# Setup of an attention block reordered: first batch normalised ahead of the second's statistics, later second queries, 40 banks of row maxima for 44

## The reference

```python
x = x + tanh(g_xattn) * xattn(layernorm(x), ctx, ctx, Wq, Wk, Wv, Wo)   # 16 heads of 8, 154 keys
x = x + tanh(g_ffn) * moe(layernorm(x), Wr, W1, b1, W2, b2)             # 8 experts, top 2, capacity 160
# xattn: softmax(where(tril, q k^T / sqrt(8), -inf)) v, then Wo
```

## Time and profile before

| | us |
|---|---|
| three timed runs | 143.20, 143.31, 143.89 |
| span of the profiled execution | 141.4 |
| PE busy / DVE busy / POOL busy / ACT busy | 125.7 / 104.8 / 85.0 / 72.9 |

### The profile page before, as it was taken

How to read it: one execution, slowest core, us unless ns; L and a number is a source line. 1 busy time by engine, 2 the same in 40 slices (tenths; PEclk the granted TensorE clock), 3 DMA queues, 4 the chain that set the end, 5 groups by cost and what they waited for, 6 DMA issues and landing times.

```text
span 141.4 us, 2256 instructions
## 1 busy us (share of the span) xinstructions
PE 125.7 (89%) x723; PEld 86.9 (61%) x723; DVE 104.8 (74%) x261; ACT 72.9 (52%) x129; POOL 85.0 (60%) x126
## 2 busy tenths in 40 slices
PE   5998988999899999999999669989979999989940
PEld 2443844456455646665258556979769999977620
...
DMA packets 19018, 12.22 MB, mean 86 GB/s; under 512 B 3381, under 2 KB 16999, under 8 KB 19008
## 3 DMA queue, kind: packets, MB, share of 16 engines
q1 hardware_dynamic: 17344, 9.59, 26.5%
...
q10 hardware_dynamic: 576, 0.66, 1.3%
...
...
## 4 chain that ended last, share of the span: by engine, by line
PE 34%; POOL 21%; issue 15%; DMA 11%; DVE 11%; ACT 2%; POOLq 2%; SPq 2%; DVEq 0%
POOL slots L536 8%; PE turn L833 6%; PE av L889 4%; DVE top L1242 4%; POOL results L568 4%; PE turn L846 3%; DMA xn_all<-results 3%; PE av L897 3%; PE sc L1120 3%; DMA X<-x 2%; PE sc L865 2%; PE turn L852 2%; DMA parts_all<-slots 2%; POOL shared L457 2%; DMA slots<-rows,slot_of 2%
## 5 line engine op out<-in xcount | busy, mean ns | idle before, releaser
L1242 DVE TENSOR_REDUCE top<-turn 128x3 fp32r<-128x462 f32 (+2 forms) x44 | 26.2, 606 | 14.1 <-PE turn L833 7.2
L568 POOL DMA_INDIRECT results<-p,result_of x18 | 19.8, 1101 | 12.9 <-DVE p L1526 8.0
L659 ACT ACTIVATE p_all<-sc 128x1024 f32<-128x1024 f32 x16 | 15.5, 1022 | 16.2 <-PE sc L865 16.1
L536 POOL DMA_INDIRECT slots<-rows,slot_of x16 | 19.4, 1211 | 6.0 <-issue 5.0
L833 PE MATMUL turn<-shared,q_all 128*128 128x462 f32 (+2 forms) x44 | 20.4, 469 | 2.3 <-DVE top L1242 0.8
L1120 PE MATMUL sc<-q_all,w_all 128*128 128x320 f32 x96 | 17.4, 320 | 1.3 <-issue 1.3
L716 ACT ACTIVATE late<-sc,B 128x320 f32<-128x320 f32 x32 | 14.9, 521 | 4.2 <-PE sc L1120 4.2
L1120 PEld LDWEIGHTS sc<-q_all,w_all 128*128 128x128 f32 x96 | 14.2, 188 | 2.3 <-issue 2.1
L833 PEld LDWEIGHTS turn<-shared,q_all 128*128 128x128 f32 x44 | 8.3, 189 | 11.3 <-ACT q_pack_all L625 4.7
L527 POOL TENSOR_SCALAR_AFFINE_SELECT p_all<-p_all 128x512 f32<-128x512 f32 x8 | 5.2, 645 | 16.8 <-ACT p_all L659 16.8
L1543 DVE TENSOR_TENSOR shared<-late,shared 128x640 fp32r<-128x640 f32 x16 | 13.1, 821 | 0.3
...
## 6 DMA issues: line engine op xcount, KB each, us to landing
...
```

The source lines that it names most:

```text
L536: nc.gpsimd.indirect_dma_start(out=slots, out_offset=bass.IndirectOffsetOnAxis(ap=slot_of[:, c:c + 1], axis=0), in_=rows[:, t, :], in_offs ...
L568: nc.gpsimd.indirect_dma_start(out=results, out_offset=bass.IndirectOffsetOnAxis(ap=result_of[0:m, e, n:n + 1], axis=0), in_=y[0:m, e % 2, ...
L659: act.activation(p0[:, t, heads, :], sc[:, heads, :], ACT.Exp, scale=SCALE).then_inc(sc_free, 1)
L1242: dve.tensor_reduce(top[:, qt, h0:h0 + nh, 3 * HD], ps[:, 0:nh * keys].rearrange("p (h k) -> p h k", h=nh), AX.X, ALU.max).then_inc(turn_f ...
```

## The change

1. VectorE normalises the first batch before it takes the second's statistics, each tile with its own signal, and TensorE transposes tile by tile. The first batch's input comes in two halves, on two queues.
2. The second batch's rows are normalised by GpSimd (4 instructions), between two pieces of masked keys. Their transposes move behind the first packing, the projection behind turn 0's last score product, and its high and low parts into turn 0.
3. The high keys are written straight from PSUM by ScalarE, with no copy in between. VectorE masks four heads' keys instead of six; GpSimd makes heads 4 to 9, then 10 to 15.
4. `slot0` and the ones beside the values are written by VectorE instead of GpSimd. The mask of the last keys is 32 x 32 and is spread by a repeated identity.
5. Units: three heads wherever possible, and head 3 of query tiles 1 to 3 in one joined bank. That is 20 banks per batch for 22; setup does 5 units instead of 7. The three units that start at head 7 stand behind turn 0's packing.
6. Fills of TensorE ahead of the first queries: 3 and 3 instead of 12 and 4.

Core of the diff:

```diff
+def units_of_maxima(b, i):
+
+    first = [(b, (0,), 4 * i, 4, P)]
+    if i == 0:
+        return first + [(b, (qt,), 0, 3, C) for qt in range(1, QT)] + [(b, tuple(range(1, QT)), 3, 1, C)]
+    starts = ((), (4, 7), (10,), (13,))[i]
+    return first + [(b, (qt,), h0, 3, C) for h0 in starts for qt in range(1, QT)]
...
-        shares = (7, 8, 6, 6, 6, 5, 5, 1)
+        maxima_todo = [u for b in range(B) for i in range(4) for u in units_of_maxima(b, i)]
+
+        shares = (5, 7, 6, 6, 6, 5, 4, 1)
         maxima_first = maxima_todo[:shares[0]]
-        FIRST_HEADS = 6
+        FIRST_HEADS = 4
+        NEXT_HEADS = 10
...
@@ -403,10 +406,8 @@
                 ins.then_inc(pool_step, 1)
                 pool.wait_ge(pool_step, steps[0])
...
+            pool.wait_ge(cleared, 1)
+            packing(pack_k, [kp for kp, qp in PRODUCTS]).then_inc(pack_ready, 1)
+            pool.tensor_copy(identb[:, :], identf[:, :]).then_inc(consts2, 1)
+            root((0, QT), 1)
             step(pool.memset(mask_q[:, :, :], 0.0))
             pool.affine_select(out=mask_q[:, :, :], in_=mask_q[:, :, :], compare_op=ALU.is_ge, fill=NEG,
-                               base=0, pattern=[[0, 4], [-1, P]], channel_multiplier=1)
+                               base=0, pattern=[[0, 4], [-1, P]], channel_multiplier=1).then_inc(consts2, 1)
             pool.tensor_copy(identr[:, :], identf[:, :])
-            pool.tensor_copy(identb[:, :], identf[:, :]).then_inc(consts2, 1)
-            root((0, QT), 1)
-            root((QT, NT), 2)
-
-            pool.wait_ge(cleared, 1)
-            packing(pack_k, [kp for kp, qp in PRODUCTS]).then_inc(pack_ready, 1)
+            pool.wait_ge(cleared, 2)
             packing(pack_q, [qp for kp, qp in PRODUCTS]).then_inc(pack_ready, 1)
...
+            pool.wait_ge(kT_ready, 1)
+            keys_for_max(0, FIRST_HEADS, NEXT_HEADS)
+
+            root((QT, NT), 2)
+            pool.wait_ge(rstd_ready, 2)
+            for t in range(QT, NT):
+                pool.tensor_scalar(xn[:, t, :], X[:, t, :], mean_var[:, t, 0:1], rstd[:, t:t + 1],
+                                   ALU.subtract, ALU.mult).then_inc(xn_ready, 1)
+            keys_for_max(0, NEXT_HEADS, H)
...
+            pool.memset(ident4[:, :, :], 0.0)
             step(pool.memset(mask_k1[:, :], 0.0))
-            for j in range(4):
-                m = mask_k1[32 * j:32 * j + 32, :]
-                step(pool.affine_select(out=m, in_=m, compare_op=ALU.is_ge, fill=NEG, base=0,
-                                        pattern=[[1, 32]], channel_multiplier=-1))
+            pool.affine_select(out=ident4[:, :, :], in_=ident4[:, :, :], compare_op=ALU.not_equal, fill=1.0, base=0,
+                               pattern=[[0, 4], [-1, 32]], channel_multiplier=1)
+            pool.affine_select(out=mask_k1[:, :], in_=mask_k1[:, :], compare_op=ALU.is_ge, fill=NEG, base=0,
+                               pattern=[[1, 32]], channel_multiplier=-1)
             pool.memset(ones[:, :], 1.0).then_inc(consts3, 1)
             pool.wait_ge(k_packed, 4)
...
+            act.dma_start(X[:, 2:QT, :], x_d[:, 2:QT, :]).then_inc(x_in[1], 16)
...
+            act.activation(kT_part[:, 0], sc1[:, 0:B * CP].rearrange("p (b k) -> p b k", b=B),
+                           ACT.Copy).then_inc(kT_ready, 1)
...
@@ -627,8 +627,7 @@
 
             act.wait_ge(k_packed, 4)
             pack(0)
-            act.wait_ge(small_in, 64)
-            act.activation(gate[:, :], G[:, :], ACT.Tanh).then_inc(gate_ready, 1)
+            turned_rows(1)
...
+                if g == 0:
+                    high_queries(1)
                 act.wait_ge(sc_full, 3 * g + 3)
                 act.activation(p1[:, t, :], sc1[:, 0:Q1], ACT.Exp, scale=SCALE).then_inc(sc_free, 1)
+                if g == 0:
+                    act.wait_ge(small_in, 64)
+                    act.activation(gate[:, :], G[:, :], ACT.Tanh).then_inc(gate_ready, 1)
...
-            fill(sc[:, 3, :], 12)
+            fill(sc[:, 3, :], 3)
             turn_rows(0)
-            fill(sc[:, 3, :], 4)
+            fill(sc[:, 3, :], 3)
+            pe.wait_ge(wq_in, 16)
             queries(0)
...
-            pe.wait_ge(consts2, 1)
+            pack_keys(1)
+            pe.wait_ge(consts2, 2)
             pe.wait_ge(kTr_first, 1)
             pe.wait_ge(q_high, 1)
-            maxima(maxima_first[0:2])
-            pack_keys(1)
+            maxima(maxima_first[0:1])
+            pack_keys(2)
+            maxima(maxima_first[1:2])
+            pack_keys(3)
             maxima(maxima_first[2:3])
-            pack_keys(2)
-            maxima(maxima_first[3:4])
-            pack_keys(3)
-            maxima(maxima_first[4:5])
-            turn_rows(1)
-            maxima(maxima_first[5:6])
             project_values()
-            maxima(maxima_first[6:])
-            queries(1)
+            maxima(maxima_first[3:])
             pe.wait_ge(pack_ready, 2)
             pe.wait_ge(q_ready, 1)
             pack(0)
-            pe.wait_ge(consts3, 1)
+            pe.wait_ge(v_ready, 5)
+            turn_rows(1)
             for g in range(NG + 2):
-                if g == 0:
-                    pe.wait_ge(kTr_ready, 1)
-                if g == 2:
-                    pe.wait_ge(kTr_ready, 2)
+                if g < 3:
+                    pe.wait_ge(kTr_ready, g + 1)
                 maxima(maxima_beside(g, 0))
                 if g < NG:
                     scores(g)
                 maxima(maxima_beside(g, 1))
                 if g == 0:
                     pe.wait_ge(k_ready, 1)
-                    pe.wait_ge(q_ready, 2)
+                    pe.wait_ge(consts3, 1)
                 if g < NG:
                     last_scores(g)
+                if g == 0:
+                    queries(1)
                 if g == NG + 1:
                     pe.wait_ge(sc_free, 3 * NG)
                     fill(sc[:, 0, :], 4)
@@ -1047,7 +1049,8 @@
                     pack(g + 1)
                 maxima(maxima_beside(g, 3))
                 if g == 1:
-                    pe.wait_ge(v_ready, 5)
+                    pe.wait_ge(ones_placed, 1)
+                    pe.wait_ge(q_ready, 2)
                 if 1 <= g <= NG:
                     values(g - 1)
                 maxima(maxima_beside(g, 4))
@@ -1197,7 +1200,7 @@
 
         @block.vector
         def _(dve):
...
-            dve.memset(pack_k_raw, 0.0)
+            dve.memset(pack_k_raw, 0.0).then_inc(cleared, 1)
             dve.memset(pack_q_raw, 0.0).then_inc(cleared, 1)
-            dve.wait_ge(x_in[0], 16)
-            statistics((0, QT), X)
-            dve.wait_ge(x_in[1], 16)
-            statistics((QT, NT), X)
-            layernorm((0, QT), X, xn, xn_ready)
-            dve.wait_ge(consts2, 1)
-            dve.tensor_reduce(minus_one[:, :], minus_raw[:, :, :], AX.XY, ALU.add).then_inc(minus_ready, 1)
+            step(dve.memset(slot0[:, :], 0.0))
+            dve.memset(slot0[:, D:D + 1], FAR).then_inc(slot_zeros, 1)
+            statistics((0, QT), X, True)
+
...
+            ones_beside_values()
+            dve.wait_ge(rstd_ready, 1)
+            for t in range(QT):
+                layernorm(t, X, xn).then_inc(xn_ready, 1)
...
-            dve.tensor_tensor(kT_part[:, 1], kT[:, :, :], kT_part[:, 0], ALU.subtract).then_inc(kT_split, 1)
+            dve.tensor_tensor(kT_part[:, 1], sc1[:, 0:B * CP].rearrange("p (b k) -> p b k", b=B), kT_part[:, 0],
+                              ALU.subtract).then_inc(kT_split, 1)
+            dve.wait_ge(consts1, 1)
             dve.tensor_tensor(kTr[:, 0, 0:FIRST_HEADS],
                               kT_part[:, 0, 0, 0:C].unsqueeze(1).to_broadcast([P, FIRST_HEADS, C]),
                               head_mask[:, :, :].rearrange("p i j -> p (i j)")[:, 0:FIRST_HEADS].unsqueeze(2)
                               .to_broadcast([P, FIRST_HEADS, C]), ALU.mult).then_inc(kTr_first, 1)
-            layernorm((QT, NT), X, xn, xn_ready)
+            dve.tensor_reduce(minus_one[:, :], minus_raw[:, :, :], AX.XY, ALU.add).then_inc(minus_ready, 1)
+            statistics((QT, NT), X, True)
...
             low_queries(0)
             dve.wait_ge(zeroed, 2)
             maxima(maxima_first)
             pass_bank()
-            low_queries(1)
 
             def after(k, n):
 
@@ -1463,11 +1478,16 @@
                     pass_bank()
                 for n in (3, 4, 5):
                     maxima(maxima_beside(g, n))
+                if g == 0:
+                    low_queries(1)
```

141 lines of the change are left out of this document (66 added, 75 removed).

## The result

| | before | after |
|---|---|---|
| four timed runs each on one chip, median (all), us | 143.60 (143.20, 143.31, 143.89, 144.82) | 148.38 (146.61, 147.87, 148.89, 150.73) |
| ratio after / before, 95% interval | | 1.0278 [1.0212, 1.0344] |
| span of the profiled execution, us | 141.4 | 148.5 |
| mean granted TensorE clock of the runs | 0.992 in the profiled one | 0.931, 0.945, 0.963, 0.967 |

The kernel became slower. The forecast was 142.4 (140.7 to 143.9); 148.38 lies outside its range, and "slower" had 0.13.

What follows compares the result with a forecast made beforehand. The prediction took TensorE, busy nearly throughout the head loop, as the bound, with two setup paths ahead of it. A, B, C and D: -3.1 + 0.6 + 0.85 + 0.8 = -0.85 from 143.31 gave 142.4 us (140.7 to 143.9).

Steps and rivals of the forecast that it cites:

- A: Setup path to the first scores, reordered and with fewer reductions: they start at 17.4 us against 20.48, -3.1 us.
- signs of "wrong": Third score product after 19.8 us, first reduction after 12.5, lower clock between 7 and 19, or gain staying near 3.
- B: TensorE's wait in turn 0 for GpSimd's block keys, before the third score product; +0.6 us.
- c: Price of each of GpSimd's four normalisations in setup; taken as 0.40 us, with 0.29 and 1.20 also considered.
- break-even, c = 0.61: Price of a GpSimd normalisation from which rival (3) decides, at a wait of 1.45 us.
- upper bound of c, 1.20 us: Highest price for a GpSimd normalisation, from a select beside VectorE's normalisation; TensorE would wait 3.8 us.
- C: Second batch's projection moved into the loop, behind turn 0's third score product; +0.85 us, ends 0.1 and 1.1.
- D: 924 columns of maxima moved from setup into the loop, two units of 0.41 us each; +0.8 us.
- Rival (1): TensorE's idle time in the loop absorbs C and D; -2.5 or -2.2 us, time 141.1; chance 0.22.
- rival (3): GpSimd's normalisation becomes the bound: at c = 1.20 the sum is +2.35 us, time 145.7; chance 0.09.
- rival (4): With fewer fills the clock falls back in setup before the maxima, 1.5 to 3 us more: about 144.5; chance 0.04.

Runs made afterwards that it cites:

- e2: The changed kernel with the second batch's normalisation on VectorE instead of GpSimd; eleven runs, median 143.71 us, ratio to before 0.9926.
- e5: The changed kernel with 8 fills in turn 0's wait for the block keys and 2 in each of three gaps behind it; median 146.53 us, ratio 1.0264.
- e3: The kernel before with only the new units of maxima and their shares; ten runs, median 144.97 us, ratio 1.0039.
- e12: The changed kernel run again, unedited, in ten runs; median 147.52 us, ratio to before 1.0111.
- e8: The changed kernel with 2 fills in each of turn 0's three gaps, the wait for the block keys left open; median 148.38 us.
- e1: The changed kernel with 8 fills only in TensorE's turn 0 wait for the block keys; four runs, median 149.42 us.
- e11: The changed kernel with the second batch's projection ahead of the wait for the block keys, not behind it; median 144.54 us, ratio to before 1.0036.
- e15: The kernel before with two needless iotas of 0.94 us delaying GpSimd ahead of its block keys; six runs, median 150.60 us, ratio 1.0491.
- e14: The same kernel as e8, on another chip; six runs, median 147.10 us, ratio to before 1.0193.
- e9: The changed kernel with the old units of maxima and the second normalisation on VectorE; twelve runs, median 144.37 us, ratio to before 1.0000.

## Why the prediction was wrong

**A held.** Forecast -3.1; the first scores came 2.93 us earlier, each step within 0.3. Of the signs of "wrong" that I named, one came: a third score product later than 19.8 (20.22).

**B failed in its size: the price c of a normalisation on GpSimd.** I took 0.40 us from the select of 128 columns; it was 0.78:

```profile
L468 POOL TENSOR_SCALAR xn_all<-X,mean_var,rstd x4: 782/782/799, 12.7 to 15.0; 128x128 f32<-128x128 f32 x4
```

VectorE reduced beside the first and half of the second, was idle from 13.85 to 14.78 us, through the rest of the second and two thirds of the third, and all four took the same. So the price belongs to the instruction, which subtracts and multiplies with one number per partition each; neither the cast (0.29) nor the select (0.40) of the earlier trace rows says anything about it. The prediction's own break-even, c = 0.61, was passed: four times 0.38 more makes the wait 1.5 us longer. It came out at 1.71 us, not 2.1, since GpSimd's other steps took 0.3 less than I had, and TensorE came there 0.16 later. The rule on the shared interfaces (the Trainium skill, GPSIMD Engine Reference, Key points) bears on none of this, as the equal durations show. The same section has VectorE about twice as fast for elementwise work; here the four took 1.34 us on VectorE (e2) for 3.13.

The upper bound of c, 1.20 us, rested on a misreading. The select of 1199 ns started at 10.2 us, and VectorE's normalisation of the first batch had ended at 9.09. What stood beside it was the product of keys and masks, with two inputs from SBUF (L1425, 9.87 to 11.11). VectorE's normalisation of the second batch stood beside the selects of 400 to 403 ns:

```profile
11.03 1.50 DVE L1235 TENSOR_SCALAR xn_all<-X,mean_var,rstd 128x128 f32<-128x128 f32 x4
...
11.33 1.12 POOL L428 TENSOR_SCALAR_AFFINE_SELECT pack_q<-pack_q 128x128 fp32r<-128x128 f32 x3
```

So the prediction's reading, that the slow selects lay beside VectorE's normalisation, is wrong; the trace agrees with that rule of the Trainium skill (GPSIMD Engine Reference, Key points) only in its case of two SBUF inputs. In the kernel after, one select of `pack_q` took 1055 ns, from 8.3 us, again beside that product (L1440, 8.26 to 9.04).

In the turns, e5 against e2, B costs 1.94 us (turn 0 of 9.11 for 7.17; the fills beside it lie in waits). Forecast +0.6. That is the first failed step, worth +1.3.

**C.** e2's turn 0 is 0.42 longer than before's with one unit fewer in it (-0.62 in e3), which leaves 1.04 for the projection. Forecast +0.85, with 1.1 as its upper end.

**D.** 0.96 us (e3) for 0.8. Rival (1), that the loop absorbs C and D, fell with these two.

**The sum without the clock.** -2.93 + 1.94 + 1.04 + 0.96 = +1.0; e5 measured +1.30 at turn 7. With c = 0.78 in it, the prediction's formula gives -3.1 + 2.1 + 0.85 + 0.8 = +0.65. This is rival (3), half-way to its price. The +1.30 make 144.6 of my 143.3, near what the change's best runs took (144.7).

**What it left out is the larger part: the clock.** This is the second failed step. The prediction's rival (4) had the clock fall in setup, for lack of fills, with a chance of 0.04. From 8 to 25.5 us it stayed at 1.00. It fell from 25.5 us, behind a turn 0 made of one wait and three gaps. In no step did I ask what a wait in the loop does to the clock: I costed the wait B at its own length, as time added once. The profiles give the fall's price by turn 4, where only the first fall lies behind: 3.92 us in the first profile of the change and 2.95 in e12, against e5, where only fills were added. In the first profile of the change a second fall at 66.5 us makes it 5.49 by turn 7. That one isn't B's: falls like it come in e8 and e2 too. Of the 7.1 us between the spans of the two profiles, before and after, 1.3 are latency and columns, 3.9 the first fall, 1.6 the second, and 0.3 lie behind the loop. That execution is the slowest of its four; over all runs the gap fills took away some 2 us of some 4.4, still more than the 1.3, and about 1 us stays unassigned.

That the fills in turn 0's gaps keep the clock up is shown by pairs of profiles that differ in those fills alone, e1 against e5 and after against e8, and by the count of mean clocks (6 of 14 and 2 of 4 without, none of 14 with). That the gaps alone decide isn't shown: e2 and e11 leave them open and mostly kept the clock, with the wait gone or cut to 0.34 us. That a delay of GpSimd suffices without the rest of the change is shown by e15. The prediction said that against (4) spoke a TensorE "still busy most of the time"; so it is ahead of 25.5 us in e1, busy for 6.10 of 7.00 us, and the clock falls.

The Trainium skill (TensorE: Matmul & The Clock Gate, What's actually happening) has the clock fall back after idle time. The traces agree only in part: in the kernel after, no idle stretch between 8 us and the fall is longer than 1.71 us, the fall comes some 5 us behind that one, and filling it didn't prevent the fall (e1), while six fills in gaps of about half a microsecond did (e5, e8, e14).

**What stays open.** What in turn 0 decides on the clock: the wait, the gaps and the new units of maxima all seem to have a part, and no run gives each its share. Why one execution of the same program seems to fall and another not (e12), while e15 falls six times in six. Why there is a later fall of some 4 us, between 60 and 112 us, at a place that moves from profile to profile, with fills or without; none of these runs tells what decides. It may be why e14's ratio, 1.019, is above the 1.009 that 1.3 us would make (the interval's lower end is 1.011): the mean clocks of its runs, 0.961 to 0.985, leave room for other falls, but only one of them was profiled. And where e9's lead of 0.5 us goes: it is still there at turn 2 (31.82 for 32.30), and is 0.28 at turn 4 and 0.03 at turn 7.
